# An adaLN transformer block: activations split to half floats as rows and transposed by DMA instead of TensorE

## What is computed

```python
h = _layernorm(x) * (1 + ca) + sa
x = x + ga * attention(h)              # 16 interleaved heads mixed, full causal, softmax over 1024
h = _layernorm(x) * (1 + cb) + sb
for l in range(2):                     # two local layers on h
    q, k, v = split(shift_token(h) @ wqkv[l])      # shift_token: the upper 128 columns come from the row before
    q, k = rotary_xpos(l2norm(q) * qs[l], l2norm(k) * ks[l])
    h = h + local_attention(q, k, v) @ wo[l]       # windows of 128 rows
    n = layernorm(shift_token(h)) * lg[l] + lb[l]
    a, g = split(n @ w1[l] + b1[l])
    h = h + (a * gelu(g)) @ w2[l] + b2[l]
x = x + gb * h
```

## Time and profile before

| | us |
|---|---|
| median of three runs | 2639.29 (2638.84 to 2642.74) |
| profiled execution, first to last instruction (span) | 2634.1 |
| PE busy in the span | 2526.7 |
| DVE busy | 2260.9 |
| ACT busy | 1935.6 |
| POOL busy | 1303.7 |

### The profile page before, as it was taken

The page is one execution under the profiler, slowest core; times in us unless marked ns, Lnnn a source line. Parts: engine busy times, 40 slices in busy tenths (PEclk is TensorE's granted clock), DMA queues, the critical chain, the costliest instruction groups (busy, mean ns, idle before and its releaser), DMA issues.

```text
span 2634.1 us, 71297 instructions
## 1 busy us (share of the span) xinstructions
PE 2526.7 (96%) x25566; PEld 1725.1 (65%) x25566; DVE 2260.9 (86%) x6247; ACT 1935.6 (73%) x4782; POOL 1303.7 (49%) x953
## 2 busy tenths in 40 slices
PE   7899989999899998999999999999999999999998
PEld 4566666666567665676656666666766666666675
DVE  8997889878898788987889878998889978799785
ACT  3698856888478784788748787587874878658884
POOL 2364535555355554555436554365544555446552
PEclk8999999999999999999999999999999999999999
DMA  5000010000100000000000000000000000000000
GB/s 192 22 7 8 5 43 3 9 5 15 33 3 9 6 17 30 4 10 4 18 29 5 8 5 20 25 6 8 6 19 25 6 8 6 20 25 6 7 6 21
DMA packets 51021, 46.45 MB, mean 18 GB/s; under 512 B 11530, under 2 KB 47980, under 8 KB 50548
## 3 DMA queue, kind: packets, MB, share of 16 engines
q1 hardware_dynamic: 50004, 40.78, 5.0%
q10 hardware_dynamic: 672, 1.10, 0.1%
HBM read 25.06 MB, written 8.42 MB: 13 GB/s over the span
## 4 chain that ended last, share of the span: by engine, by line
PE 69%; DVE 12%; ACT 8%; issue 5%; POOL 4%; DMA 1%; SPq 1%; DVEq 0%; POOLq 0%; ACTq 0%
PE ps L508 10%; PE ps L613 9%; PE ps L581 8%; PE ps L547 6%; PE ps L514 5%; PE ps L617 4%; PE ps L565 4%; PE ps L524 3%; PE ps L594 3%; PE ps L160 2%; PE ps L162 2%; PE ps L161 2%; ACT ar_b L808 2%; PE ps L461 2%; PE ps L407 2%
## 5 line engine op out<-in xcount | busy, mean ns | idle before, releaser
L808 ACT ACTIVATE ar_b<-ar_b,small 128x192 f32<-128x192 f32 (+1 forms) x1024 | 445.2, 437 | 50.4 <-DVE small L1100 48.6
L1366 POOL TENSOR_TENSOR small<-small,neg_half 128x16 f32<-128x16 f32 x128 | 382.2, 2986 | 121.8 <-DVE small L1059 119.9
L1370 POOL TENSOR_TENSOR ar_c<-ar_c 128x1024 f32<-128x1024 f32 x128 | 302.7, 2365 | 282.3 <-DVE ar_c L1086 281.7
L1100 DVE CUSTOM_DVE_ANT_0 ar_b<-ps,mask_t,small 128x192 f32<-128x192 f32 x896 | 319.3, 413 | 29.7 <-PE ps L547 29.2
L1385 POOL TENSOR_TENSOR mlp<-mlp 128x512 f16<-128x512 f32 x160 | 196.3, 1231 | 200.5 <-ACT mlp L863 199.3
L508 PE MATMUL ps<-wqkv_hi,ht_hi 128*128 128x512 f16 x768 | 292.2, 381 | 0.0
L508 PE MATMUL ps<-wqkv_lo,ht_hi 128*128 128x512 f16 x768 | 291.1, 379 | 0.0
L613 PE MATMUL ps<-ht_hi,w_hi 128*128 128x512 f16 (+1 forms) x704 | 268.2, 381 | 5.5 <-ACT ht_hi L759 5.5
L613 PE MATMUL ps<-ht_hi,w_lo 128*128 128x512 f16 (+1 forms) x704 | 267.1, 379 | 0.0
L581 PE MATMUL ps<-ar_b,ar_a 128*64 128x128 f32 x3840 | 239.4, 276 | 0.5 <-DVE ar_b L1124 0.3
L294 POOL TENSOR_SCALAR stats<-stats 128x2 f32<-128x2 f32 x128 | 33.2, 260 | 407.6 <-DVE stats L1149 312.5
(11 more groups left out here) (193 smaller groups left out, 6673.3 us busy)
## 6 DMA issues: line engine op xcount, KB each, us to landing
xu<-in_L_attn_x_dram SPq DMA_DIRECT2D x32, 256.0 KB, 2.8
out_dram<-xu SPq DMA_DIRECT2D x64, 128.0 KB, 2.4
rows<-xu SPq DMA_DIRECT2D x128, 63.5 KB
mlp<-in_L_ffn_wqkv_dram SPq DMA_DIRECT2D x2, 1536.0 KB, 6.4
modb<-mod_rows SPq DMA_DIRECT2D x8, 384.0 KB, 4.5
rows<-in_L_ffn_w_dram SPq DMA_DIRECT2D x2, 1364.0 KB, 9.5
rows<-xu SPq DMA_DIRECT2D x112, 0.5 KB
ar_b<-in_L_wmod_dram SPq DMA_DIRECT2D x2, 768.0 KB, 7.4
```

Of the source, the lines that this page charges most:

```text
L808: last = act.activation(pw, pw, ACT.Exp, bias=mnw[:, n % 2, h:h + 1], scale=-1.0, accum_out=smw[:, n % 2, h:h + 1])
L1100: dve.tensor_tensor_reduce(out=PW[:, pw_at(f, q, i) + c:pw_at(f, q, i) + KW], in0=ps[:, bk, i * KW + c:(i + 1) * KW], in1=mask, scale=rinv ...
L1366: pool.tensor_tensor(rinv[:, n % 4, :], ssm[:, n % 2, :], neg_half[:, 0:16], ALU.pow).then_inc(s_rinv, 1)
L1370: pool.tensor_tensor(M1[:, n % 2, :], M1[:, n % 2, :], M2, ALU.add).then_inc(s_add, 1)
```

## The change

- `ht` becomes one tensor `ht_all` with the halves beside each other, and its first row is at place 16 (`HT0`) instead of 1.
- `D` and `N` leave PE's list, and with them 128 PSUM bank uses. `dh` on ACT writes `hi` of the two row tiles of `U` to `d_rows` (float16, rows on partitions), `dl` on DVE writes the rest beside it. `nh` and `nl` do the same from `XN` to `n_rows`. All read SBUF instead of PSUM.
- `D` and `N` are now on SP's list: after `dl` or `nl`, and after the readers of the old contents of `ht`, SP issues two transposing DMAs, each of one tile's rows, 128 partitions x 512 half floats (128 KB).
- `E` waits for the landing of its pair (and of the pair before), once, ahead of all six matmuls; before it waited for `hi` first and for `lo` ahead of the last two. `Wg`, `Wa` likewise.
- `d_rows`, `n_rows` and now also `XN` have one buffer: `dh` and `nh` wait for the landing of the transposes of the pair before, `lk` for `nl` of the pair before.
- The begin times are all new: `PERIOD` is 321.65, `EDGE` holds more of the first batches, and the setup's loads are at other times.

```diff
-        ht = [sb(f"ht_{s}", [P, NC, SEQ + 1], F16) for s in ("hi", "lo")]
+        ht_all = sb("ht", [P, 2, NC, HT0 + SEQ], F16)
+        ht = [ht_all[:, s] for s in range(2)]
+        d_rows = sb("d_rows", [P, 2, 2, DIM], F16)
...
-        XN = rows[:, 0:1024].rearrange("p (r t n) -> p r t n", r=2, t=2)
+        XN = rows[:, 0:512].rearrange("p (t n) -> p t n", t=2)
+        n_rows = rows[:, 512:1024].bitcast(F16).rearrange("p (t s n) -> p t s n", t=2, s=2)
...
+        h_landed = lambda L: 16 * (4 * L + 2)
+        ln_landed = lambda L: 16 * (4 * L + 4)
...
@@ sync @@
+                    elif k == "D":
+                        L, p = piece[1:]
+                        sp.wait_ge(s_dl, at("dl", L, p))
+                        if L % DEPTH:
+                            sp.wait_ge(s_w1g, at("Wg", L - 1, p // 2, NJ))
+                            sp.wait_ge(s_w1, at("Wa", L - 1, p // 2, NJ - 1))
+                        else:
+                            sp.wait_ge(s_proj, at("pj", L // DEPTH, 2 * p + 1))
+                        for t in range(2):
+                            c = HT0 + (2 * p + t) * P
+                            sp.dma_start_transpose(ht_all[:, :, :, c:c + P].rearrange("p s c n -> p (s c) n"),
+                                                   d_rows[:, t].rearrange("p s n -> p (s n)")).then_inc(s_hT[p], 16)
+                    elif k == "N":
+                        L, p = piece[1:]
+                        sp.wait_ge(s_nl, at("nl", L, p))
+                        for k2 in range(3):
+                            sp.wait_ge(s_qkv, at("E", L * NT + min(2 * p + 2, NT - 1), k2))
...
@@ tensor @@
-                    elif k == "D":
...
-                        bk = claim(pe, *piece)
-                        rows_t(bk, lambda t: U[:, 2 * p + t, :]).then_inc(s_dt, 1)
-                    elif k == "N":
...
-                        rows_t(bk, lambda t: XN[:, p % 2, t, :]).then_inc(s_nt, 1)
                     elif k == "E":
-                        pe.wait_ge(s_dh, at("dh", L, w // 2))
+                        if w and w % 2 == 0:
+                            pe.wait_ge(s_hT[w // 2 - 1], h_landed(L))
+                        pe.wait_ge(s_hT[w // 2], h_landed(L))
...
-                        pe.wait_ge(s_dl, at("dl", L, w // 2))
...
                     elif k in ("Wg", "Wa"):
-                        pe.wait_ge(s_nh, at("nh", L, 2 * g + 1))
+                        for p in (2 * g, 2 * g + 1):
+                            pe.wait_ge(s_hT[p], ln_landed(L))
...
-                        pe.wait_ge(s_nl, at("nl", L, 2 * g + 1))
...
@@ scalar @@
                     elif k == "dh":
-                        act.wait_ge(s_dt, at("D", L, p))
...
+                        if L or p:
+                            M, q = divmod(L * 4 + p - 1, 4)
+                            act.wait_ge(s_hT[q], h_landed(M))
+                        act.activation(d_rows[:, :, 0, :], U[:, 2 * p:2 * p + 2, :], ACT.Copy).then_inc(s_dh, 1)
                     elif k == "nh":
+                        act.wait_ge(s_xnw, at("lk", L, p))
+                        if L or p:
+                            M, q = divmod(L * 4 + p - 1, 4)
+                            act.wait_ge(s_hT[q], ln_landed(M))
+                        act.activation(n_rows[:, :, 0, :], XN, ACT.Copy).then_inc(s_nh, 1)
...
@@ vector @@
+                        dve.tensor_tensor(d_rows[:, :, 1, :], U[:, 2 * p:2 * p + 2, :], d_rows[:, :, 0, :],
+                                          ALU.subtract).then_inc(s_dl, 1)
...
+                        dve.tensor_tensor(n_rows[:, :, 1, :], XN, n_rows[:, :, 0, :], ALU.subtract).then_inc(s_nl, 1)
...
-                        if L or p >= 2:
-                            dve.wait_ge(s_nt, at("N", *divmod(L * 4 + p - 2, 4)))
+                        if L or p:
+                            dve.wait_ge(s_nl, at("nl", *divmod(L * 4 + p - 1, 4)))
...
-PERIOD = 316.98
+PERIOD = 321.65
+    ("D", "sp"): {(0, 0): 73.91, (0, 1): 99.47, (0, 2): 118.1, (0, 3): 124.87, (1, 0): 201.63, (1, 1): 220.59,
+        (1, 2): 265.53, (1, 3): 285.85},
+    ("N", "sp"): {(0, 0): 159.59, (0, 1): 172.17, (0, 2): 210.18, (0, 3): 235.22, (1, 0): 284.02, (1, 1): 299.22,
+        (1, 2): 345.38, (1, 3): 357.5},
...
```

## The result

The changed kernel takes 3001.5 us (3001.1 to 3004.6, four runs) against 2639.8 us: ratio 1.1373, 95% interval 1.1357 to 1.1389. It is 362 us slower. The forecast was 2631 us, and the range ended at 2690.

A forecast was written before the change was run, and what follows sets the result against it. PE, 96% busy, was taken as the bound, with about a third of the path latency between engines. Per batch -7.0 for transposes and +6 for gaps made -1.0, -8 us over eight batches: 2639.3 to 2631 us, range 2585 to 2690.

The forecast's parts named there:

- Transposes leave PE: Line 407's transposes, 128 steps of 0.44 us on the path: 56 us gained, 7.0 per batch.
- Splits at nothing: dh, nh, dl and nl reading SBUF instead of PSUM: no gain or loss taken, 5 us either way for dl and nl.
- SP: 256 new transposing DMAs on SP's queue, issues 0.60 to 0.94 us: nothing taken; pair latency 3.3 us, bounds 1.9 and 5.7.
- nine near pairs: Nine of a batch's 16 transposed pairs, issued only 3.85 to 4.85 us ahead of their matmuls; none waits at 3.3 us.
- What the longer path gives back: PE's gaps in a steady batch, read from the order tables: 20 us old, 26 new, so 6 us lost per batch.
- Setup and last batch at nothing: Rearranged setup and shorter last batch: both taken as no change in time.
- Late landings: Rival: landings beyond 4.24 us stop PE at nine tight pairs per batch, 72 us per further us, up to 2736 us; 30%.
- Block by block: Rival: transposes move in small pieces and land like the slowest load, 9.5 us; about 3010 us; 4%.
- Nothing happens: Rival: DVE, busy 278 of 321 us, sets the batch and PE's 7 us turn idle; 2639 us; 8%.
- the gain stays: Rival: the order covers landings of 2 to 3 us and all 56 us stay; 2583 us, half 2611; 20%.
- The last sentence of the prediction: SP's queue: if transposes' issues last much longer than others, the shifts and loads behind them become late; no size given.

The follow-up runs named there:

- h_half: Kernel before with each of the 512 float32 transposes of D and N replaced by a 128x128 half-float identity product, activations left out: 2619.2 us, ratio 0.9925.
- f_slack8: Kernel before, its order kept, with only the eight of sixteen D and N steps per batch that have 6.6 us or more of room by DMA: 2677.1 us.
- g_few: Kernel before, its order kept, with only five of sixteen D and N steps per batch by DMA: 2656.7 us, ratio 1.0073.
- a_split: Changed kernel, new order kept, with the row shift's DMA of 127 partitions issued as two, of 112 and 15: 2853.9 us, ratio 1.0809.
- c_pe: Code of the kernel before (transposes on PE, splits from PSUM, two buffers) with the changed kernel's tables of begin times: 2999.5 us, ratio 1.1354.
- e_dn: Kernel before, order kept but splits moved, with all D and N steps by DMA, one buffer of rows, two of XN: 2918.3 us, ratio 1.1055.

## Why the prediction was wrong

**Transposes leave PE, 56 us.** Right in kind. By `h_half` 0.77 of PE's time there is on the path (19 of 24.7), some 43 us; in the new order with a quick shift the step was worth 38.

**Splits at nothing.** Right in their length: `dl` and `nl` together take 92.2 us (681 and 759 ns) against 87.3. What their new places on ACT and DVE do to others was not in the sum; in the old order `f_slack8` and `g_few` lose 37 and 18.5 us in which PE waits for no landing to speak of.

**SP.** "Issues last 0.60 to 0.94 us" was short for this kind: a transposing DMA holds the queue 1.27 us in the median. Landing was right, 2.5 us against 2.4 in the rows. A pair so takes 3.85 us where 3.3 was taken, inside the bounds of 1.9 and 5.7, and just what the new table counts (3.85 to 4.85 at the nine near pairs).

**What the longer path gives back, 6 us per batch.** This is the step that failed, and with it the row shift, whose place in the new order the prediction put at nothing. PE's gaps were read off the new table, with the shortest distance between two kinds of pieces taken as their duration. Such a sum takes over whatever the table assumes, and one assumption is wrong: 1.91 us for the row shift, which needs 5.1. It also has no footing in the trace: for the old table it gives 20 us of gaps per batch, where PE was idle 9.2. I had two ways to see the wrong assumption. The old table's 4.71 against the new 1.91 stood in the same diff; I compared `X` loads (4.17 and 2.95), found that the two tables assume different durations, and drew only that their periods can't be compared. And in the earlier trace rows I took the wrong pair of rows: the read at 1306.24 belongs to the pair before, so "a shift was read 1.27 us after its issue began" is no bound at all. The reader of a shift has to be found by its tile. Measured, the longer path and the order gave back 16.0 + 32.3 = 48.3 us per batch, eight times the term. Of the 362 us the late shift alone is 148 (`a_split`), and `c_pe` has the loss without the longer path, so it is the order and not the way through SP.

**Setup and last batch at nothing.** The setup cost some 38 us more. Nothing in the argument had looked at the loads' order, which was changed as well.

**A term that was missing: the clock.** Idle time was counted at its own length. In the kernel after PE's clock is 0.96 in a steady batch, 0.99 before, which is some 11 of the 16 us by which PE's remaining work lasts longer per batch.

**The rivals.** *Late landings* put the loss at nine near pairs and asked for 70 us or more of waits of `E`, `Wg`, `Wa`; there are at most 46, and `c_pe` loses the same without any landing. The mechanism is real in another order: it is 199 of the 279 us that `e_dn` loses. *Block by block* gave about 3010 us, near the result, by a mechanism that is refuted: a pair lands in 3.85 us, not in 9.5, so the nearness is luck. By the first of the two rules of the Trainium skill ("VectorE: DVE Perf Modes", section "The three transpose paths", 1309 ns for a block of 128x128) eight blocks would take an estimated 10.5 us; the trace, with 3.85, does not agree. With the second ("Advanced Engine Details and Errata", section "X-Bar Transpose (TRN2)", as fast as ordinary DMAs) it does for the landing (2.5 against 2.4 us), not for the issue (1.27 against 0.33 to 0.94). *Nothing happens* and *the gain stays* are out. The last sentence of the prediction, that the shifts could become late, named the right transfer and the wrong cause: its 5.1 us are as long as before, and `c_pe`, with no transpose on SP's queue, is as slow.

**Open.** Of the 214 us that a quick shift leaves, some 40 are setup. In a steady batch of `a_split` (344.3 us) PE is busy 315.6 and idle 28.7 us. The idle time is spread over many small waits: 51 us in the whole run end with a landing, the others are for ACT, DVE and POOL, no group of them above 27 us; which of the new table's distances are too short was not tried one by one.

## What to carry to other kernels

When a change brings a new hand-made or searched order with it, the order is the larger part of the change until shown otherwise: run the old mechanism in the new order and the new mechanism in the old one before anything is said of the mechanism. A new step put into an old order shifts its neighbours too: look for the wait that takes the old one's place. Compare the distances that two orders keep between a transfer's issue and its reader with what the trace measures, for every kind of transfer, also those that the change does not touch. Count an idle stretch of TensorE of some microseconds at more than its length, and keep a step on TensorE where the order leaves its replacement less room than its whole latency.

## What the runs showed of the hardware

**127 partitions in one DMA.** 63.5 KB in 127 partitions are read at the earliest 5.1 us after the begin of the issue; as 112 and 15 partitions, 2.7 us after the first of the two. Other counts were not tried.

**Transposing DMAs.** 128 x 512 half floats from SBUF to SBUF: issue 1.27 us and landing 2.5 us in the median, up to 2.8 and 5.5.

**DVE held up by POOL.** DVE's 107 us more are the same instructions lasting longer; the largest part, 44 us, lies with one line. It is an operation on 128x16 numbers (`ss`); min/median/max in ns, in the kernel before and in the kernel after:

```profile
L1059 DVE TENSOR_SCALAR small<-small x128: 174/175/714, 107.9 to 2552.2; 128x16 f32<-128x16 f32 x128
```

```profile
L1063 DVE TENSOR_SCALAR small<-small x128: 174/175/2081, 130.5 to 2909.3; 128x16 f32<-128x16 f32 x128
```

The timeline of the kernel after has one that takes 0.17 us and one of 1.08 us, which ends as POOL's long product does (1596.70 + 2.89 = 1599.59):

```profile
1586.66 0.17 DVE L1063 TENSOR_SCALAR small<-small 128x16 f32<-128x16 f32 x1
...
1596.70 2.89 POOL L1373 TENSOR_TENSOR ar_c<-ar_c 128x1024 f32<-128x1024 f32 x1
1597.30 1.21 DVE L1058 TENSOR_REDUCE small<-ar_c 128x16 f32<-128x1024 f32 x1
1598.54 1.08 DVE L1063 TENSOR_SCALAR small<-small 128x16 f32<-128x16 f32 x1
```

The reduction beside it is not held up (1.21 us, as elsewhere), so it depends on the operation. In the new order these two fall together more often: 48 of the 128 last over 0.3 us in the kernel after and 15 before, and every one of them ends within 0.04 us after an operation of POOL. The line takes 74.7 us in the kernel after and 30.8 before, and `c_pe`, with before's code, has 68.7. The Trainium skill, "Trainium Architecture — The Big Picture", section "What this means for kernel authors", says that on the engines' side of SBUF only the port pair shared by these two is contended for, and that it is an exclusive lock; the rows agree for this operation.
